# Denominators of an attention block by half images: 16 narrow products in four quadrants instead of 8 in two

## The reference

```
h = conv8x8(norm(concat(x, 4 shifts of x)) * gamma + beta) + b     # 64 images, 169 tokens, 128 wide
x = layernorm(h);  q, k, v = split(x @ Wqkv.T), 8 heads of 64
q_prime = exp(q * 64**-0.5 @ proj.T);  k_prime = exp(k @ proj.T)
D = q_prime @ k_prime.sum(tokens)                                  # 8 denominators for each token
out = (q_prime @ (k_prime.T @ v)) * 1 / (D + 1e-6);  h = h + out @ Wout.T + bout
x = layernorm(h);  h = h + sum over the top 2 of 8 experts of gate * (silu(x @ W) * (x @ V)) @ W2
```

## Time and profile before

| | |
|---|---|
| median of three runs | 1265.29 us (1262.27 to 1266.17) |
| the profiled execution | 1265.36 us, its span 1263.6 us |
| instructions | 29487 |
| mean granted clock of PE | 0.962 of full speed |
| PE busy in the span | 1134.4 us (90%) |
| DVE busy in the span | 890.2 us (70%) |

### The profile page before, as it was taken

How to read it: one execution, slowest core, us unless ns; L and a number is a source line. 1 busy time by engine, 2 the same in 40 slices (tenths; PEclk the granted TensorE clock), 3 DMA queues, 4 the chain that set the end, 5 groups by cost and what they waited for, 6 DMA issues and landing times.

```text
span 1263.6 us, 29487 instructions
## 1 busy us (share of the span) xinstructions
PE 1134.4 (90%) x8352; PEld 954.4 (76%) x8353; DVE 890.2 (70%) x3191; ACT 573.9 (45%) x1317; POOL 601.4 (48%) x655
## 2 busy tenths in 40 slices
PE   4669999989999999999999962899999999999994
PEld 3647666767667667666677652899999999999994
DVE  5437778778777787787886667577777777777773
ACT  1453443534534434435333331555555555555552
POOL 0001443535443435344435445366666666666664
PEclk9589999999999999999999986899999999999998
DMA  8105121020020111210101004244444443443442
GB/s 153 45 19 169 32 58 40 28 71 31 28 73 24 54 42 37 61 37 23 36 21 38 26 30 134 44 56 53 55 53 56 52 56 53 55 54 51 58 52 26
DMA packets 87661, 65.77 MB, mean 52 GB/s; under 512 B 25915, under 2 KB 79995, under 8 KB 87583
## 3 DMA queue, kind: packets, MB, share of 16 engines
q0 software_dynamic: 32704, 24.99, 13.9%
q1 hardware_dynamic: 54878, 39.83, 12.7%
HBM read 33.07 MB, written 31.71 MB: 51 GB/s over the span
## 4 chain that ended last, share of the span: by engine, by line
PE 43%; DVE 4%; issue 3%; POOL 2%; DMA 1%; SPq 1%; ACT 0%; POOLq 0%; DVEq 0%; ACTq 0%
PE bank L1204 21%; PE bank L1216 13%; PE bank L563 2%; PE bank L1192 2%; PE bank L635 1%; DMA out_rows<-yo,dest 1%; POOL sorted_rows L1114 1%; PE bank L628 1%; PE bank L622 1%; PE bank L510 1%; DVE attn L788 1%; DVE patches L754 1%; DVE wl_all L1252 1%; DVE xtok L838 0%; POOL rstd L1095 0%
## 5 line engine op out<-in xcount | busy, mean ns | idle before, releaser
L1345 POOL DMA_INDIRECT out_rows<-yo,dest x184 | 301.7, 1640 | 168.5 <-issue 117.3
L1114 POOL DMA_INDIRECT sorted_rows<-xrow_all,sloti x192 | 192.1, 1000 | 233.2 <-DVE sloti L926 186.8
L1204 PE MATMUL bank<-xT_e,wv 128*128 128x256 f32 x2208 | 290.0, 287 | 0.9 <-DVE xT_e L1296 0.9
L1204 PEld LDWEIGHTS bank<-xT_e,wv 128*128 128x128 f32 x2208 | 273.0, 190 | 1.3 <-DVE xT_e L1296 1.3
L1303 DVE TENSOR_TENSOR hid<-sil,bank 128x256 f32<-128x256 f32 x368 | 155.2, 422 | 84.9 <-ACT sil L1274 65.6
L1274 ACT ACTIVATE sil<-bank 128x256 f32<-128x256 f32 x368 | 141.5, 385 | 161.5 <-PE bank L1204 138.9
L1216 PE MATMUL bank<-w,hid 128*128 x1472 | 179.5, 275 | 1.0 <-DVE hid L1303 1.0
L1216 PEld LDWEIGHTS bank<-w,hid 128*128 128x128 f32 x1472 | 171.5, 192 | 1.2 <-issue 1.2
L754 DVE TENSOR_TENSOR patches<-bank,gam 128x416 f32<-128x416 f32 (+3 forms) x160 | 103.8, 756 | 27.4 <-PE bank L460 24.3
L1031 ACT ACTIVATE attn<-bank 128x256 f32<-128x256 f32 x128 | 49.5, 386 | 152.1 <-PE bank L611 113.6
L1259 ACT CAST wv<-wv_all 128x1024 fp32r x92 | 96.3, 1047 | 40.5 <-issue 40.5
(11 more groups left out here) (183 smaller groups left out, 1944.4 us busy)
## 6 DMA issues: line engine op xcount, KB each, us to landing
xr<-sorted_rows SPq DMA_DIRECT2D x92, 130.0 KB
raw<-in_x SPq DMA_DIRECT2D x64, 84.5 KB
raw<-in_x SPq DMA_DIRECT2D x128, 39.0 KB
out_rows<-attn SPq DMA_DIRECT2D x64, 64.0 KB
sorted_rows<-xrow_all,sloti POOLq DMA_INDIRECT x192
out_rows<-yo,dest POOLq DMA_INDIRECT x184
wv_all<-in_L_ffn_W SPq DMA_DIRECT2D x8, 256.0 KB, 5.3
wv_all<-in_L_ffn_V SPq DMA_DIRECT2D x8, 256.0 KB, 5.4
```

Source lines behind the costliest of these rows:

```text
L1114: po.indirect_dma_start(sorted_rows, bass.IndirectOffsetOnAxis(sloti[:, pd, j, ch:ch + 1], 0), xrow[:, pd, j, ch], None).then_inc(s(f"scat ...
L1204: q = pe.matmul(bank[fc][:, TT * m:TT * m + TT], wv[:, p, w_, m, cols], xT[:, p, x_], start=(w_ + x_ == 0), stop=(w_ == 1))
L1345: po.indirect_dma_start(out, bass.IndirectOffsetOnAxis(dest[:, p, a:a + 1], 0), yo[:, p, a], None, compute_op=ALU.add).then_inc(s(f"added{ ...
```

## The change

Each image's 169 tokens are taken in two halves, tokens 0 to 85 and 84 to 168. The denominators of the first half of both images go to rows 0 and 32 of bank 7 as before, those of the second half to rows 64 and 96. So there are 16 products of 86 or 85 columns where there were 8 of 169, with weights of 32 columns, 24 of them zero, so that all 128 rows of bank 7 are written. The addition, the reciprocal, the copies and the subtractions become 86 columns wide on 128 or 64 rows, at the same count of instructions. `rparts` has two slices, one for each half, and each broadcast is two products for each image, of 86 and 84 columns, with the same weights: 16 products a step where there were 8. `mm` grows from 136 to 160 columns for each slice; a memset at setup zeroes the added ones and waits for the last beta patch, whose source lies in the same memory; PE waits for it once. The fill of `rparts` with zeros goes.

```
-                        for i in range(2):
-                            t = pe.matmul(bank[7][32 * i:32 * i + HEADS, 0:TOK], mm[:, pc, i, j, D:],
-                                          qf[:, pc, j, TOK * i:TOK * i + TOK], start=(j == 0), stop=(j == 3))
+                        for hf, (first, _) in enumerate(FIRST):            # FIRST = [(0, 0), (84, 2)]
+                            for i in range(2):
+                                quad, n_ = 32 * (2 * hf + i), PART - hf    # PART = 86
+                                t = pe.matmul(bank[7][quad:quad + SUMS, 0:n_], mm[:, pc, i, j, D:],
+                                              qf[:, pc, j, TOK * i + first:TOK * i + first + n_], start=(j == 0), stop=(j == 3))
...
-                        t = pe.matmul(bank[(7, 1)[j % 2]][:, (TOK + 1) * i:(TOK + 1) * (i + 1)], pick_head[:, i, j], rparts[:],
-                                      start=True, stop=True)
+                        for hf, (first, skip) in enumerate(FIRST):
+                            at = (TOK + 1) * i + first + skip
+                            t = pe.matmul(bank[(7, 1)[j % 2]][:, at:at + PART - skip], pick_head[:, i, j], rparts[0:104, hf, skip:],
+                                          start=True, stop=True)
...
-                    ve.tensor_scalar(dsum[:], bank[7][0:40, 0:TOK], 1e-6, None, ALU.add).then_inc(s("dsum_ready"), 1)
+                    ve.tensor_scalar(dsum[:], bank[7][:, 0:PART], 1e-6, None, ALU.add).then_inc(s("dsum_ready"), 1)
                     ve.reciprocal(rden[:], dsum[:]).then_inc(s("rden_whole"), 1)
-                    for r in (0, 32):
-                        t = ve.tensor_copy(rparts[r:r + HEADS, 0:TOK], rden[r:r + HEADS])
+                    for u in range(2):
+                        t = ve.tensor_copy(rparts[64 * u:64 * u + 64, u, 0:PART], rden[64 * u:64 * u + 64])
-                    for r in (0, 32):
-                        t = ve.tensor_tensor(rparts[64 + r:64 + r + HEADS, 0:TOK], rden[r:r + HEADS],
-                                             rparts[r:r + HEADS, 0:TOK].bitcast(F32), ALU.subtract)
+                    for u in range(2):
+                        t = ve.tensor_tensor(rparts[64 - 64 * u:128 - 64 * u, u, 0:PART], rden[64 * u:64 * u + 64],
+                                             rparts[64 * u:64 * u + 64, u, 0:PART].bitcast(F32), ALU.subtract)
...
-            ve.tensor_copy(rparts[:], zeros[0:104, 0:TOK + 1])
+            ve.wait_ge(s("beta_patched"), 5)
+            ve.memset(mm[:, :, :, :, D + HEADS:], 0.0).then_inc(s("sums_zero"), 1)
```

More of the change, by code:

```diff
@@ L38 @@
 NTRASH = 4 * 128
+SUMS = 32
+PART = TOK // 2 + 2
+FIRST = [(0, 0), (TOK // 2, 2)]
 NSTAT = 5 * C * S * S
@@ L161, in tokens @@
         xT = sb("xT", [128, 2, 2, NCH * 128], F32R)
-        attn = sb("attn", [128, 8 * PT + 6 * HEADS * NF + 16 * (D + HEADS) + 8 * D])
+        attn = sb("attn", [128, 8 * PT + 6 * HEADS * NF + 16 * (D + SUMS) + 8 * D])
         taken = [0]
@@ L172, in tokens @@
         gT = piece(2 * HEADS * NF).rearrange("p (i n) -> p i n", i=2)
-        mm = piece(16 * (D + HEADS)).rearrange("p (s i j n) -> p s i j n", s=2, i=2, j=4)
+        mm = piece(16 * (D + SUMS)).rearrange("p (s i j n) -> p s i j n", s=2, i=2, j=4)
         h2 = piece(2 * NCH * D).rearrange("p (s c n) -> p s c n", s=2, c=NCH)
         braw = attn[0:NP1, 0:5 * C * PATCH * S].rearrange("p (c k x) -> p c k x", c=5 * C, k=PATCH)
-        dsum = sb("dsum", [40, TOK])
-        rden = sb("rden", [40, TOK])
-        rparts = sb("rparts", [104, TOK + 1], F32R)
+        dsum = sb("dsum", [128, PART])
+        rden = sb("rden", [128, PART])
+        rparts = sb("rparts", [128, 2, PART], F32R)
         xrow_all = sb("xrow_all", [128, 16 * RW])
@@ L475, in _ @@
             pe.wait_ge(s("gate_centred"), 1)
+            pe.wait_ge(s("sums_zero"), 1)
             def step(n, k, g, par, a, b, c, d, fr):
@@ L1025, in m_copy @@
                     ac.wait_ge(s("m_done"), 4 * mb + f + 1)
-                    ac.copy(mm[:, pb, i, 2 * jj:2 * jj + 2],
+                    ac.copy(mm[:, pb, i, 2 * jj:2 * jj + 2, 0:D + HEADS],
                             bank[(6, 1)[jj]][:, 0:2 * (D + HEADS)].rearrange("p (j n) -> p j n", j=2)).then_inc(s("m_evac"), 1)
```

## The result

The changed kernel takes 1343.99 us, the median of four runs (1334.67 to 1345.56), against 1264.82 us for the kernel before on the same chip (four runs): ratio 1.0618, 95% interval 1.0598 to 1.0639. It is 6.2% slower; the forecast was 1266.0 us, range 1259 to 1279.

A forecast was written before the change was run, and what follows sets the result against it. PE bounds first (626.9 of 677 us busy), though POOL, ACT or DVE set some stretches. Terms by kind of step, waits, tail and setup sum to +0.6 us on 1265.4: 1266.0 us, range 1259 to 1279.

The forecast's parts named there:

- DVE (L804 to L813): Reciprocal chain after the denominators: narrower instructions take 0.84 us a step less on DVE, mostly hidden under the convolution.
- k = 2: Five steps with image loads, PE waiting 1.11 us at L530: -0.04 to +0.5 each, middle taken, +1.0 us in all.
- k = 1: Six steps with an image shift: POOL's root keeps its place, broadcasts exceed slack, +0.07 us each, +0.4 in all.
- k = 0: Six steps with image sums: part of the broadcasts' cost hides in the wait for ACT, -0.33 us each, -2.0 in all.
- Denominators on PE: L510: four quadrants stream side by side, 1.25 us to the convolution becomes 0.70, gain 0.55 us a step.
- four quadrants don't overlap further: Rival at L510: only two quadrants overlap, the stretch stays at 1.25 us, 1278.5 us in all; chance 0.15.
- starts can't come that close: Rival at L510: record starts at least 0.03 us apart, the stretch takes 1.10 us, 1274.5 in all; chance 0.08.
- the same at its upper end: Rival at L510: record starts at least 0.058 us apart on the mean, 1.97 us, 1298 in all; chance 0.05.
- Broadcasts on PE: L487: eight more products, paced by weight loads 0.11 us apart, lose 0.88 us a step.
- the second load is free: Rival at L487: a second load of the same weights costs nothing, so broadcasts stay as they are, 1252.5 us; chance 0.12.
- k = 3: Seven steps with pieces, all on PE: denominators' gain less broadcasts' cost, +0.33 us each, +2.3 in all.
- plain ones: Six steps without sums, shift, loads or pieces: gain and cost about cancel, about 0.

The follow-up runs named there:

- before_behind: Kernel before, with a wait on POOL so a pair's last four scatters are issued only after the next step's denominators are signalled: 1275.25 us.
- spread_halved: Kernel before, with each broadcast product cut into two of 86 and 84 columns, 16 for 8: +14 us, ratio 1.0115.
- after_root_first: Changed kernel, with four scatters behind the next step's denominators' signal and POOL's image root moved ahead of them: 1252.7 us.
- whole_root_first: Changed kernel, quadrants kept, broadcasts back to 170 columns, scatters behind the denominators' signal, POOL's image root ahead of them: 1240.2 us, ratio 0.9829.
- before_root_first: Kernel before, with four scatters behind the next step's denominators' signal and POOL's image root moved ahead of them: 1257.8 us.
- sums_halved: Kernel before, with each denominator product cut into two of 85 and 84 columns, in the same two quadrants, 32 records: 1325.49 us.

## Why the prediction was wrong

**The step that failed** is in "DVE (L804 to L813)": "After, dsum starts 0.55 earlier, its chain would end 1.4 earlier". It takes for granted that DVE sees the denominators' signal when they end. In the kernel before it does within 0.02 to 0.6 us outside the k = 2 steps with loads, so the sum had no term for it, and no rival had it either; with twice the records it comes 2.6 to 5.1 us late in 22 of 32 steps. "And the convolution, only 0.55 earlier, sets L820" failed with it, since the convolution's signal is 2.2 us late in k = 1. The steps before n = 5 and the k = 0 ones came out near their forecasts; the rest lost 78 us.

**A clue was in hand.** "What DVE waits for I can't name", said of k = 2: L530's 1.11 us were this effect at the convolution's signal, raised 1.4 to 1.5 us behind its record. before_behind removed it (7.1 to 1.8 us of waits). I took the middle of two bounds, -0.04 and +0.5, where the unnamed cause was one that the change would make larger. Its size by the loads was misread as well: n = 2 has the same loads, was counted as plain, and has no such wait; it has no scatter.

**Denominators on PE: right.** 0.73 us to the convolution for a forecast of 0.70. The starts of the 32 records go in rounds 0.073 to 0.099 us apart, and inside a round, with four quadrants, one start is 0.000 to 0.010 behind the other. So the rivals "four quadrants don't overlap further", "starts can't come that close" and "the same at its upper end" are all wrong. The Trainium skill ("TensorE: Matmul & The Clock Gate", "Wait — 56ns, not 53.3ns?"), whose least distance of about 25 ns I had quoted, is not borne out between quadrants here; and by the factor of 2.38 for three tiles in "Measured speedup vs the span model" the stretch would have been 0.84, where 0.73 was measured.

**Broadcasts on PE: right as a price (+14 us in spread_halved), a little high as a size.** From L540 to L573 the changed kernel needs 5.41 us in undisturbed steps, forecast 5.5, before 4.9 to 5.0. So the rival "the second load is free" is wrong too. Taking the price away was worth 12.5 us (after_root_first to whole_root_first), once nothing else set the steps.

**DVE's part: right and hidden as forecast**: 0.69 us for the reciprocal, a chain 0.84 us shorter than in most steps before (1.95 for 2.79), and L540 at 4.67 us after the first denominator where 4.65 was forecast.

**The kinds of steps**, with the denominators' signals on time (after_root_first less before_root_first): k = 0 -0.35 us (forecast -0.33); k = 1 -0.2 (+0.07); k = 2 -0.6 in eight steps together (middle of -0.04 and +0.5 a step); k = 3 -0.1 a step (+0.33; but in n = 3, before any scatter, +0.27); plain ones -0.2 (0). The sum over n = 2 to 31 is -5.3 us, mine was +0.6 with the tail. In k = 3 it is again a late signal that makes the difference: before_root_first needs 11.0 us to L563 there, where the step that I priced has 10.54, and the 0.5 us are the first k product's signal, shown above. Without it these steps would come to about +0.3, as forecast (an estimate: -0.15 + 0.49). By this estimate some 3 us of the 5 that after_root_first is ahead are late signals at another place, and not the products.

**The clock** had no term either. With the same products PE is busy 1180.0 us in the changed kernel and 1141.0 in after_root_first: 39 us go to the lower clock after the waits (0.93 of full speed for 0.99 over the steps), about as much as the 35.5 us of added idle time.

The range missed by 65 us because it took in bounds for each cost that I had listed, and none for the assumption between them.

## What to carry to other kernels

Splitting products into more and shorter ones can cost far more than their own time when POOL issues scatters beside them: count PE's records in each stretch that lies beside scatters, and ask what waits for the signal at its end. In a profile an idle time with an unnamed releaser is to be followed up with the time at which the semaphore was raised, before it is given a price. When a wait is added on a queue, as here on POOL, look first at what stands behind it: moving the image root ahead of the scatters was worth 14 us in the changed kernel and 17 in the one before, the whole change 5.

## What the runs showed of the hardware

PE's semaphores are mostly raised 0.014 us after the modelled end of their record (0.05 for the denominators in four quadrants). Beside scatters it is another matter: in the changed kernel the denominators' is 3.0 us late in k = 1 and 4.6 to 5.1 in k = 2 with loads, and in k = 1 the next ones (convolution, q products) come together at about 6.04 to 6.09 us from the first denominator. DVE's and ACT's own semaphores in the same stretches are raised 0.009 to 0.012 us after their instructions; only PE's are late. In these runs the delay grows with the number of records in the burst (32: 0.2 us in k = 1; 64: 2.4 to 3.0) and with the number of scatters over it (0, 2, 4: 0, 2.3, 3.0 us in k = 1), and image loads that SP issues beside scatters add some 2 us. Loads alone, with the DMA engines 96% busy, delayed nothing. Order, quadrants and width of weights made no difference to this beyond which of the two places k = 3 took (sums_halved always the earlier, 3.8).

The Trainium skill ("TensorE: Matmul & The Clock Gate", "The cost: per-tile semaphore tail") gives a model of the tail behind packed products; for four tiles and one increment it makes 0.07 us, an estimate from that page, near the 0.05 measured without scatters, and it has nothing for 3 to 5 us. "Perfetto Trace Analysis" ("Per-instruction lifecycle: what the profiler-reported window actually captures") says that a signal's way lies outside an instruction's window; the traces agree, since no instruction's row shows the delay.

What stays open: what PE's signals wait for, and whether it is the scatters' issue on POOL or their own packets that holds them up; no run separates the two. And every run here, timed ones too, has its granted clock recorded, so that no run tells whether recording has a part in it, in the delay or in the 6.2%.
